# Normalising tiles as soon as they are complete, and writing out the middle groups of two attentions

## The chip, the core and the metric

The kernel runs on one core of a Trainium2 chip. The core has five engines that run side by side and wait for one another through semaphores: TensorE (PE in the profile; the loading of its weights is PEld), VectorE (DVE), ScalarE (ACT), GpSimd (POOL), and SyncE (SP), which here only issues DMA transfers. The metric is the time of one execution on the device, in microseconds (us).

## The reference, cut to what matters

Two decoder layers on 1024 tokens (4 sequences of 256) of width 512. Each layer is an attention and a feed-forward network, and after each of the four the residual sum is normalised over the 512 columns:

```
def _layernorm(x, axis=-1, eps=1e-05):
    m = jnp.mean(x, axis=axis, keepdims=True)
    v = jnp.var(x, axis=axis, keepdims=True)
    return (x - m) / jnp.sqrt(v + eps)

x = L0_attn_hidden_states
x = _layernorm(x + _L0_attn_ref(x, ...), axis=-1)   # 32 heads over a latent of 64, causal
x = _layernorm(x + _L0_ffn_ref(x, ...), axis=-1)    # weights unpacked from 4 bits (GPTQ)
x = _layernorm(x + _L1_attn_ref(x, ...), axis=-1)   # 32 heads and 32 latent heads, causal
x = _layernorm(x + _L1_ffn_ref(x, ...), axis=-1)    # weights rounded to 16 values per block of 64 (NF4)
```

## The kernel before

**Data.** `X` holds the tokens in SBUF as 8 tiles of 128 tokens by 512 columns (`TT` = 8), two tiles for each of the four sequences. `XT` is the same transposed. Every float32 matrix is held as a pair `hi` and `lo` (its rounded part and the rest), and each product is three matmuls (`product`, L59 to L65, so all of them carry lines 63, 64 and 65).

**Blocks.** The program is a row of blocks, and every engine meets every other at the end of each: an opening load; `transposed_block` (t0); the latent projections; the first attention (layer 0); `gptq_block`, which unpacks weights; `transposed_block` (t1); the first feed-forward; `transposed_block` (t2); `latent_query_block`; the second attention (layer 1), which also rounds the weights of the last feed-forward; `nf4_block`; `transposed_block` (t3); the second feed-forward; `transposed_block` (t4), which only normalises; and the store of the result.

**`transposed_block`** (L79 to L140). DVE takes the statistics of all eight tiles (L99, L102), adds epsilon (L104); ACT takes the root (L122); DVE takes the reciprocal (L106) and normalises the tiles in place (L109). PE transposes each tile in four matmuls (L139) as soon as it is normalised, into one of two PSUM banks; ACT copies the bank to `XT.hi` (L126), DVE writes the rest to `XT.lo` (L114), and only then is the bank free. t0 transposes without normalising.

**The attentions.** Both run over groups of heads, 4 groups in the first and 8 in the second, and each group over 16 steps (4 sequences by 4 heads or pairs of heads). A step n does the scores of n, the outputs of earlier steps, and projections for later ones. On every engine the first and the last group are written out, and the middle ones are a hardware loop, in which every count that a semaphore is compared with is computed in a register:

```
        def groups(eng, body):
            body(0, True, False)
            with eng.Fori(1, L0_GROUPS - 1) as g:
                body(g, False, False)
            body(L0_GROUPS - 1, False, True)
```

So the loop of the first attention runs twice and jumps back once, that of the second runs six times and jumps back five times. Where a wait needs a register, `hold` adds a semaphore increment behind it. After the last step of a sequence, `add_output` adds two tiles of the sum of a group to `X` (L759 in the first attention, L1396 in the second). In the last group this completes tiles 0 and 1 at step 6, 2 and 3 at step 10, 4 and 5 at step 14, and 6 and 7 at the very end.

**In the second attention**, POOL sums the terms of the rounded weights (L1076); at the first step of a group and at three later ones, DVE finishes a piece when POOL's sums are done (`code_end`, L1405) and starts the next (`code_start`), ahead of the reciprocal (L1378) that the step's softmax needs.

**The feed-forwards** (`ffn_block`) run over the two halves of the tokens; DVE adds the four tiles of the first half to `X` in the middle of the block (`add(0)`, unit 11 of 22) and the other four at its end.

Of the kernel before, what the change touches and what calls it, by code (L numbers as in the profile page):

```python
# [16 lines left out]
P = 128  # L17
# [61 lines left out]
def transposed_block(nc, tag, X, XT, ident, banks, signals, normed, flipped):  # L79


    with ExitStack() as ctx:  # L82
        sb = lambda n, s, d: ctx.enter_context(nc.sbuf_tensor(tag + n, s, d))
        stats = sb("stats", [P, TT, 6], F32)
        moments = sb("moments", [P, TT, 2], F32)
        root = sb("root", [P, TT], F32)
        inverse = sb("inverse", [P, TT], F32)
        stats_done, moments_done, var_ready, root_ready, inverse_done, x_ready, turned, hi_done, lo_done = signals
        normalise = normed is not None
        block = ctx.enter_context(nc.Block())  # L90

        def bank_view(t):
            return banks[t % 2][:, :].rearrange("p (k c) -> p k c", k=KT)

        @block.vector
        def _(dve):
            if normalise:
                for t in range(TT):
                    dve.bn_stats(stats[:, t, :], X[:, t, :]).then_inc(stats_done, 1)  # L99
                for t in range(TT):  # L100
                    dve.wait_ge(stats_done, TT * normed + t + 1)
                    dve.bn_aggr(moments[:, t, :], stats[:, t, :]).then_inc(moments_done, 1)  # L102
                dve.wait_ge(moments_done, TT * (normed + 1))
                dve.tensor_scalar(root[:, :], moments[:, :, 1], EPS, None, ALU.add).then_inc(var_ready, 1)  # L104
                dve.wait_ge(root_ready, normed + 1)
                dve.reciprocal(inverse[:, :], moments[:, :, 1]).then_inc(inverse_done, 1)  # L106
                dve.wait_ge(inverse_done, normed + 1)
                for t in range(TT):
                    dve.tensor_scalar(X[:, t, :], X[:, t, :], moments[:, t, 0:1], inverse[:, t:t + 1],  # L109
                                      ALU.subtract, ALU.mult).then_inc(x_ready, 1)  # L110
            if XT is not None:
                for t in range(TT):
                    dve.wait_ge(hi_done, TT * flipped + t + 1)
# [16 lines left out]
        def _(pe):  # L130
            if XT is None:
                return
            for t in range(TT):
                if normalise:
                    pe.wait_ge(x_ready, TT * normed + t + 1)
# [1799 lines left out]
```

## Time and profile before

| what | value |
|---|---|
| median of 3 timed runs | 2655.54 us (2655.51, 2655.54, 2663.71) |
| the profiled execution's own time | 2663.52 us |
| its span, first to last instruction | 2661.7 us |
| busy: PE, PEld, DVE, ACT, POOL | 89%, 78%, 66%, 55%, 59% |
| mean granted TensorE clock | 0.931 of full speed |
| idle of PE before t1, t2, t3 (from the last matmul before) | 9.02, 9.55, 7.67 us |
| from the last sum of the last feed-forward to the end of the span | 17.8 us |

The profile's page divides the span into 40 slices. PE is busy nearly throughout except in the slices of the opening, of the weight unpacking after the first attention, of the start of the second attention, of `nf4_block` and of the end. A line number such as L109 is a line of the kernel before. "x8" counts instructions, and what stands in square brackets is how long the engine was idle before, and which instruction ended that wait.

### The profile page before, as it was taken

How to read it: one execution, taken by the hardware profiler on the slowest of the kernel's cores; microseconds unless marked ns; L12 is line 12 of the kernel's file. 1: busy time of each engine (PE TensorE's matmuls, PEld its weight loads, DVE VectorE, ACT ScalarE, POOL GpSimd, SP SyncE). 2: the span in 40 equal slices, each digit the busy share in tenths (PEclk: the TensorE clock that was granted, in tenths of full speed). 3: DMA queues.
4: the chain of work that ended last, by engine and by line, in shares of the span. 5: the costliest groups of instructions: out<-in, count | busy, mean ns of one | idle time of the engine just before them, and what ended most of it. 6: DMA issues, size and time to landing. Idle time of an engine off the chain costs nothing. (4 is left out here: it accounts for less than half of the span.)

```text
span 2661.7 us, 44610 instructions
## 1 busy us (share of the span) xinstructions
PE 2371.4 (89%) x14333; PEld 2070.7 (78%) x14333; DVE 1756.2 (66%) x3123; ACT 1469.0 (55%) x3970; POOL 1564.7 (59%) x1320
## 2 busy tenths in 40 slices
PE   6699999996679957999999999999999999986996
PEld 5588888885358837889888888888888988875885
DVE  2366656664951136888888888888888888862123
ACT  1266656664033315666767767667676676764332
POOL 0636353631024408788787877878878878750542
PEclk8699989998579978999999999999999999997998
DMA  1201010101000012011111110111101111003000
GB/s 47 67 16 48 13 38 17 44 5 40 0 0 1 0 35 62 28 58 44 35 49 36 46 57 24 53 40 46 53 17 59 44 40 47 22 5 135 0 1 32
DMA packets 41237, 93.68 MB, mean 35 GB/s; under 512 B 4724, under 2 KB 6648, under 8 KB 39696
## 3 DMA queue, kind: packets, MB, share of 16 engines
q1 hardware_dynamic: 40980, 90.55, 10.6%
q8 instruction: 126, 2.06, 0.3%
q14 instruction: 131, 1.07, 0.1%
HBM read 79.78 MB, written 10.75 MB: 34 GB/s over the span
## 5 line engine op out<-in xcount | busy, mean ns | idle before, releaser
L1076 POOL TENSOR_TENSOR a_nf_acc<-a_nf_acc,a_nf_term 128x512 f32<-128x512 f32 (+1 forms) x416 | 587.5, 1412 | 141.3 <-ACT a_nf_term L1162 76.9
L1510 POOL TENSOR_TENSOR f_w_lo<-WGU,f_w_hi 128x512 fp32r<-128x512 f32 x88 | 113.1, 1288 | 370.5 <-ACT f_w_hi L1526 370.5
L1122 ACT ACTIVATE a_probs<-bank,a_dip 128x128 f32<-128x128 f32 (+1 forms) x512 | 208.8, 420 | 193.7 <-DVE a_dip L1372 193.7
L1131 ACT ACTIVATE a_probs<-a_probs,a_share 128x128 f32<-128x128 f32 (+1 forms) x512 | 191.9, 459 | 61.7 <-DVE a_share L1378 61.7
L1057 POOL TENSOR_TENSOR a_qk_lo<-a_straight,a_qk_hi 128x512 fp32r<-128x512 f32 (+1 forms) x160 | 194.5, 1217 | 32.1 <-ACT a_qk_hi L1108 32.1
L63 PE MATMUL bank<-a_wo_hi,a_ot_hi 128*128 128x512 f32 x512 | 212.7, 415 | 0.0
L1442 DVE TENSOR_SCALAR a_nf_term<-a_nf_unit 128x512 f32<-128x512 f32 (+1 forms) x288 | 205.4, 758 | 3.4 <-DVE a_nf_unit L1425 0.6
L1553 DVE TENSOR_TENSOR f_hidden<-bank,f_act_gate 128x512 f32<-128x512 f32 x44 | 30.4, 692 | 263.2 <-PE bank L65 257.2
L65 PE MATMUL bank<-a_wo_hi,a_ot_lo 128*128 128x512 f32 x512 | 201.3, 393 | 0.0
L64 PE MATMUL bank<-a_wo_lo,a_ot_hi 128*128 128x512 f32 x512 | 199.7, 390 | 0.0
L450 POOL TENSOR_TENSOR a_straight<-a_straight,a_crossed 128x512 f32<-128x512 f32 x64 | 82.5, 1289 | 191.0 <-DVE a_crossed L717 191.0
L1108 ACT ACTIVATE a_qk_hi<-a_straight 128x512 fp32r<-128x512 f32 (+1 forms) x160 | 94.5, 590 | 176.4 <-DVE a_straight L1357 176.4
L1263 PE MATMUL bank<-ident,a_probs 128*128 128x128 f32 x768 | 134.2, 284 | 50.5 <-DVE a_pt_lo L1383 49.6
L508 ACT ACTIVATE a_probs<-bank,a_dip 128x128 f32<-128x128 f32 (+1 forms) x256 | 104.3, 420 | 134.4 <-DVE a_dip L735 134.4
L63 PE MATMUL bank<-a_wvk_hi,XT_hi 128*128 128x320 f32 x512 | 169.5, 331 | 0.1
L1383 DVE TENSOR_TENSOR a_pt_lo<-bank,a_pt_hi 128x384 fp32r<-128x384 f32 x256 | 140.7, 550 | 40.4 <-ACT a_pt_hi L1139 40.4
L65 PE MATMUL bank<-a_wvk_hi,XT_lo 128*128 128x320 f32 x512 | 160.9, 314 | 0.0
L64 PE MATMUL bank<-a_wvk_lo,XT_hi 128*128 128x320 f32 x512 | 160.7, 314 | 0.0
L1357 DVE TENSOR_TENSOR a_straight<-a_straight,a_crossed 128x512 f32<-128x512 f32 (+1 forms) x160 | 153.9, 962 | 5.5
L1263 PEld LDWEIGHTS bank<-ident,a_probs 128*128 128x128 f32 x768 | 85.7, 142 | 83.6 <-DVE a_pt_lo L1383 74.8
L65 PE MATMUL bank<-XT_hi,a_wql_lo 128*128 128x256 f32 x512 | 146.5, 286 | 0.0
L64 PE MATMUL bank<-XT_lo,a_wql_hi 128*128 128x256 f32 x512 | 146.5, 286 | 0.0
(247 smaller groups left out, 8618.2 us busy)
## 6 DMA issues: line engine op xcount, KB each, us to landing
a_raw<-in_l_o SPq DMA_DIRECT2D x64, 256.0 KB, 2.6
a_raw<-in_l_vk SPq DMA_DIRECT2D x32, 384.0 KB, 3.1
a_raw<-in_l_ql SPq DMA_DIRECT2D x32, 320.0 KB, 2.9
a_raw<-in_l_ou SPq DMA_DIRECT2D x32, 288.0 KB, 2.7
n_codes<-coded_w SPq DMA_DIRECT2D x8, 1056.0 KB, 12.7
a_raw<-in_l_nr SPq DMA_DIRECT2D x16, 384.0 KB, 3.0
a_nf_raw<-in_w_nf SPq DMA_DIRECT2D x24, 256.0 KB, 2.6
coded_w<-a_nf_acc SPq DMA_DIRECT2D x24, 256.0 KB, 2.1
```

The lines of the kernel that those rows point to most:

```text
L63: pe.matmul(out, lh, rh, start=first, stop=False)
L64: pe.matmul(out, lh, rl, start=False, stop=False)
L65: return pe.matmul(out, ll, rh, start=False, stop=last)
L1057: pool.tensor_tensor(rope_cell(name, QK.lo), src, rope_cell(name, QK.hi).bitcast(F32), ALU.subtract)\
L1076: pool.tensor_tensor(acc, left, nf_term[:, i % CODE_RING, 0:w], ALU.add).then_inc(nf_added, 1)
L1122: act.activation(probs[:, n % 2, col:col + keys], bank[:, at:at + keys], ACT.Exp, bias=dip[:, n % 2, i:i + 1], accum_out=total[:, n % 2, i ...
L1131: ins = act.activation(cell, cell, ACT.Copy, scale=share[:, n % 2, i:i + 1])
L1263: last_ = pe.transpose(TURN[:, i * P:(i + 1) * P], probs[:, n % 2, col:col + P], ident[:, :])
L1357: dve.tensor_tensor(row, row, crossed[:, 0:n], ALU.add).then_inc(rope_sum, 1)
L1383: dve.tensor_tensor(PT.lo[:, at], TURN[:, 0:3 * P], PT.hi[:, at].bitcast(F32), ALU.subtract)\
L1442: dve.tensor_scalar(nf_term[:, i % CODE_RING, 0:w], nf_unit[:, 0:w], -BOUNDS[k], JUMPS[k], ALU.is_ge, ALU.mult).then_inc(nf_terms, 1)
L1510: pool.tensor_tensor(lo, src, hi.bitcast(F32), ALU.subtract).then_inc(part_lo[i], 1)
```

## The change

**Normalisation.** The buffers and semaphores of the normalisation now live through the whole program (`norm_buffers`), and its steps are functions (`measure`, `variance`, `deviation`, `normalise`) that take a range of tiles and a part, 0 or 1. In the last group of each attention DVE measures two tiles after each of three `add_output`s, ACT takes the root for six tiles in the tail of the group, and DVE normalises those six before its last `add_output`. In both feed-forwards DVE measures the four tiles of the first half at unit 11 and normalises them at unit 14. The `transposed_block`s normalise only what is left: two tiles in t1 and t3, four in t2. They use four PSUM banks in turn in place of two, and `low(0)` stands ahead of the normalisation. In the last feed-forward the first half of the result is stored while the second is computed, and `last_block` normalises the other four tiles and stores each as it is done.

**Groups.** In both attentions `for g in range(...)` stands in place of the hardware loop, on every engine: the middle groups are written out, with constants in place of registers, and `hold` adds no increment. `mask` of the second attention shares its place in SBUF with `probs`.

```diff
+def normalise(dve, X, norm, normed, part, tiles):
+    at = slice(tiles[0], tiles[-1] + 1)
+    dve.wait_ge(norm["root_ready"], 2 * normed + part + 1)
+    dve.reciprocal(norm["inverse"][:, at], norm["moments"][:, at, 1]).then_inc(norm["inverse_done"], 1)
+    dve.wait_ge(norm["inverse_done"], 2 * normed + part + 1)
+    for t in tiles:
+        dve.tensor_scalar(X[:, t, :], X[:, t, :], norm["moments"][:, t, 0:1], norm["inverse"][:, t:t + 1],
+                          ALU.subtract, ALU.mult).then_inc(norm["x_ready"], 1)
...
-            return banks[t % 2][:, :].rearrange("p (k c) -> p k c", k=KT)
+            return banks[t % 4][:, :].rearrange("p (k c) -> p k c", k=KT)
...
+            if normed is not None:
+                measure(dve, X, norm, normed, late)
+                variance(dve, norm, normed, late)
+                low(0)
+                normalise(dve, X, norm, normed, 1, late)
+            for t in range(0 if normed is None else 1, TT):
+                low(t)
...
+            high(0)
+            if normed is not None:
+                deviation(act, norm, normed, 1, late)
+            for t in range(1, TT):
+                high(t)
...
-                if t >= 2:
-                    pe.wait_ge(lo_done, TT * flipped + t - 1)
+                if t >= 4:
+                    pe.wait_ge(lo_done, TT * flipped + t - 3)
...
+def last_block(nc, X, out, norm, normed, stored):
+    late = range(TT // 2, TT)
...
+            for t in late:
+                sp.wait_ge(norm["x_ready"], TT * normed + t + 1)
+                sp.dma_start(out[t * P:(t + 1) * P, :], X[:, t, :]).then_inc(stored, 16)
...
         def groups(eng, body):
             body(0, True, False)
-            with eng.Fori(1, L0_GROUPS - 1) as g:
+            for g in range(1, L0_GROUPS - 1):
                 body(g, False, False)
             body(L0_GROUPS - 1, False, True)
...
+                    deviation(act, norm, normed, 0, range(TT - 2))
                     out_high(L0_STEPS - 1)
...
                         add_output(n - 3)
+                        if last and n > PAIRS:
+                            tiles = range(2 * (n // PAIRS) - 2, 2 * (n // PAIRS))
+                            dve.wait_ge(out_free, 2 * (BATCH * g + n // PAIRS))
+                            measure(dve, X, norm, normed, tiles)
...
                 if last:
+                    variance(dve, norm, normed, range(TT - 2))
                     out_low(L0_STEPS - 2)
                     for a in range(NP):
                         probs_low(L0_STEPS - 1, a)
                     out_low(L0_STEPS - 1)
+                    normalise(dve, X, norm, normed, 0, range(TT - 2))
                     add_output(L0_STEPS - 1)
...
-            with eng.Fori(1, GROUPS - 1) as g:
+            for g in range(1, GROUPS - 1):
...
+                if u == FT + 1:
+                    deviation(act, norm, normed, 0, range(HT))
...
                     add(0)
+                    dve.wait_ge(added, HT)
+                    measure(dve, X, norm, normed, range(HT))
+                if u == FT + 1:
+                    variance(dve, norm, normed, range(HT))
+                if u == FT + 3:
+                    normalise(dve, X, norm, normed, 0, range(HT))
```

DVE, block t1, before: the statistics, the normalisation and the low parts of all eight tiles stand in a row (`t_` names the block's own buffers).

```order
L99 BN_STATS t_stats<-X 128x6 x8
L102 BN_AGGR t_moments<-t_stats 128x2 x8
L104 TENSOR_SCALAR t_root<-t_moments 128x8
L106 RECIPROCAL t_inverse<-t_moments 128x8
L109 TENSOR_SCALAR X<-X,t_moments,t_inverse 128x512 x8
L114 TENSOR_TENSOR XT_lo<-bank,XT_hi 128x4x128 x8
```

DVE, the same block in the changed kernel (`ln_` names the shared buffers, lines are those of the changed kernel):

```order
L90 BN_STATS ln_stats<-X 128x6 x2
L93 BN_AGGR ln_moments<-ln_stats 128x2 x2
L100 TENSOR_SCALAR ln_root<-ln_moments 128x2
L137 TENSOR_TENSOR XT_lo<-bank,XT_hi 128x4x128
L115 RECIPROCAL ln_inverse<-ln_moments 128x2
L118 TENSOR_SCALAR X<-X,ln_moments,ln_inverse 128x512 x2
L137 TENSOR_TENSOR XT_lo<-bank,XT_hi 128x4x128 x7
```

Six of the eight tiles have left the block, and the first low part is ahead of the two that are normalised. They have gone, for t1, into the tail of the first attention. DVE there, in the changed kernel:

```order
L100 TENSOR_SCALAR ln_root<-ln_moments 128x6
L805 TENSOR_TENSOR a_ot_lo<-bank,a_ot_hi 128x256
L800 TENSOR_TENSOR a_pt_lo<-bank,a_pt_hi 128x384 x2
L805 TENSOR_TENSOR a_ot_lo<-bank,a_ot_hi 128x256
L115 RECIPROCAL ln_inverse<-ln_moments 128x6
L118 TENSOR_SCALAR X<-X,ln_moments,ln_inverse 128x512 x6
L813 TENSOR_TENSOR X<-bank,X 128x512 x2
```

The seven new instructions (reciprocal and six tiles) stand between the last `a_ot_lo` and the last sum. ACT, from the tail of the first attention to the first feed-forward, in the changed kernel:

```order
L584 ACTIVATE a_ot_hi<-bank 128x256
L578 ACTIVATE a_pt_hi<-bank 128x384 x2
L108 ACT_TABLE_LOAD
L108 ACTIVATE ln_moments<-ln_root 128x6
L584 ACTIVATE a_ot_hi<-bank 128x256
L368 UNCONDITIONAL_BRANCH
L149 UNCONDITIONAL_BRANCH
L153 ACTIVATE XT_hi<-bank 128x4x128
L108 ACTIVATE ln_moments<-ln_root 128x2
L153 ACTIVATE XT_hi<-bank 128x4x128 x7
```

The load of the table for the root has moved from the start of t1 into the attention's tail, and t1 itself has none.

## Rows read from the trace of the kernel before

**Rows 1.** Waits of PE: engine, line, waited for: us in total, times, longest
```profile
PE bank L139 <- DVE X L109: 26.2, 3, 9.5
PE bank L63 <- issue: 14.0, 6, 3.1
```

**Rows 2.** Timeline of t1: start us, us, engine, line, operation, count [idle before <-releaser]
```profile
745.86 4.84 DVE L99 BATCH_NORM_STATS2 t_stats<-X 128x6 f32<-128x512 f32 x8 [0.33 <-PEq L1596]
...
751.96 3.74 DVE L109 TENSOR_SCALAR X<-X,t_moments,t_inverse 128x512 f32<-128x512 f32 x8
752.56 1.99 PE L139 MATMUL bank<-ident,X 128*128 128x128 f32 x8 [9.02 <-DVE X L109]
753.73 0.60 ACT L126 ACTIVATE XT_hi<-bank 128x512 fp32r<-128x512 f32 x1 [2.04 <-PE bank L139]
754.59 0.60 ACT L126 ACTIVATE XT_hi<-bank 128x512 fp32r<-128x512 f32 x1 [0.26 <-PE bank L139]
755.62 1.28 DVE L114 TENSOR_TENSOR XT_lo<-bank,XT_hi 128x512 fp32r<-128x512 f32 x2
...
764.28 0.69 DVE L114 TENSOR_TENSOR XT_lo<-bank,XT_hi 128x512 fp32r<-128x512 f32 x1 [0.16 <-ACT XT_hi L126]
```

**Rows 3.** Timeline of t0, its start and its last low part
```profile
9.92 1.28 ACT L126 ACT_TABLE_LOAD   x1 [9.92 <-PEq L1788]
...
20.33 0.69 DVE L114 TENSOR_TENSOR XT_lo<-bank,XT_hi 128x512 fp32r<-128x512 f32 x1 [0.16 <-ACT XT_hi L126]
```

**Rows 4.** DMA issues: out<-in, queue, count, KB each, us to landing
```profile
coded_w<-a_nf_acc SPq DMA_DIRECT2D x24, 256.0 KB, 2.1
...
out_x<-X SPq DMA_DIRECT2D x1, 2048.0 KB, 7.0
```

**Rows 5.** Timeline of DVE, tail of the first attention
```profile
646.16 0.42 DVE L751 TENSOR_TENSOR a_ot_lo<-bank,a_ot_hi 128x256 fp32r<-128x256 f32 x1 [3.21 <-ACT a_ot_hi L531]
648.54 1.29 DVE L759 TENSOR_TENSOR X<-bank,X 128x512 f32<-128x512 f32 x2 [1.95 <-PE bank L65]
```

**Rows 6.** Timeline of DVE, tail of the second attention
```profile
2399.17 0.75 DVE L1405 SCALAR_TENSOR_TENSOR a_nf_acc<-a_nf_acc,a_nf_top 128x576 f32<-128x576 f32 x1
2403.43 1.29 DVE L1396 TENSOR_TENSOR X<-bank,X 128x512 f32<-128x512 f32 x2 [3.52 <-PE bank L65]
```

**Rows 7.** Windows (length, busy and count by engine, clock): second attention, last group; first feed-forward
```profile
2286.60:2328.70 42.10, 40.66 (x274) 36.85 (x273) 38.26 (x67) 31.18 (x86) 31.21 (x24) 1.00 0.05 15
...
860.00:900.00 40.00, 40.00 (x178) 33.10 (x178) 9.41 (x14) 13.72 (x25) 19.36 (x15) 1.00 0.00 1
```

**Rows 8.** Windows in the first attention: step 15 to step 1, and steps 4 to 11
```profile
360.59:386.70 26.11, 23.26 (x121) 20.15 (x120) 11.24 (x24) 10.84 (x35) 14.18 (x21) 0.74 0.13 36
501.95:519.68 17.73, 17.29 (x121) 14.74 (x120) 11.13 (x24) 10.93 (x35) 11.74 (x16) 1.00 0.13 35
140.30:201.38 61.08, 59.46 (x402) 50.35 (x402) 40.16 (x76) 40.16 (x129) 23.80 (x23) 1.00 0.02 7
272.84:334.46 61.62, 59.50 (x403) 50.40 (x402) 40.16 (x76) 40.16 (x129) 23.73 (x22) 1.00 0.03 8
```

**Rows 9.** Windows in the second attention, step 15 to step 13 of the next group
```profile
1346.25:1499.45 153.20, 145.54 (x960) 133.50 (x959) 130.46 (x231) 103.06 (x284) 120.87 (x96) 0.98 0.13 40
...
2034.20:2186.62 152.42, 144.23 (x960) 132.02 (x959) 131.66 (x231) 103.13 (x284) 120.40 (x96) 0.99 0.13 40
2205.49:2359.99 154.50, 145.44 (x961) 133.02 (x959) 134.28 (x231) 102.89 (x284) 112.33 (x90) 0.98 0.08 27
1174.08:1327.38 153.30, 144.07 (x961) 131.84 (x960) 131.70 (x231) 103.15 (x284) 120.68 (x96) 0.99 0.12 39
```

**Rows 10.** Timeline of DVE and PE at two group boundaries of the second attention
```profile
1364.48 1.31 DVE L1405 SCALAR_TENSOR_TENSOR a_nf_acc<-a_nf_acc,a_nf_top 128x576 f32<-128x576 f32 x1
...
2223.29 1.83 DVE L1405 SCALAR_TENSOR_TENSOR a_nf_acc<-a_nf_acc,a_nf_top 128x576 f32<-128x576 f32 x1 [2.10 <-POOL a_nf_acc L1076]
...
2228.87 0.90 PE L1263 MATMUL bank<-ident,a_probs 128*128 128x128 f32 x3 [3.98 <-DVE a_pt_lo L1383]
```

More of the change, by code:

```diff
@@ L90, in transposed_block @@
+def transposed_block(nc, X, XT, ident, banks, signals, norm, normed, flipped, early):
+    with ExitStack() as ctx:
+        turned, hi_done, lo_done = signals
+        late = range(early, TT)
         block = ctx.enter_context(nc.Block())
         def bank_view(t):
-            return banks[t % 2][:, :].rearrange("p (k c) -> p k c", k=KT)
+            return banks[t % 4][:, :].rearrange("p (k c) -> p k c", k=KT)
         @block.vector
         def _(dve):
[L97 to L110, printed above, removed]
@@ L123, in _, with high @@
-            if XT is not None:
-                for t in range(TT):
-                    act.wait_ge(turned, TT * flipped + t + 1)
-                    act.activation(XT.hi[:, :, t * P:(t + 1) * P], bank_view(t), ACT.Copy)\
-                       .then_inc(hi_done, 1)
+            def high(t):
+                act.wait_ge(turned, TT * flipped + t + 1)
+                act.activation(XT.hi[:, :, t * P:(t + 1) * P], bank_view(t), ACT.Copy)\
+                   .then_inc(hi_done, 1)
+            high(0)
@@ L1462, in body @@
                         add_output(n - 3)
+                        if last and n > PER:
+                            tiles = range(2 * (n // PER) - 2, 2 * (n // PER))
+                            dve.wait_ge(out_free, 2 * (BATCH * g + n // PER))
+                            measure(dve, X, norm, normed, tiles)
                     for name in units[1:]:
@@ L1465, in body @@
                 if last:
+                    variance(dve, norm, normed, range(TT - 2))
                     out_low(STEPS - 2)
@@ L1470, in body, with ffn_block @@
                     code_end(PER - 1)
+                    normalise(dve, X, norm, normed, 0, range(TT - 2))
                     add_output(STEPS - 1)
             groups(dve, body)
-def ffn_block(nc, tag, X, XT, banks, WGU, WD):
+def ffn_block(nc, tag, X, XT, banks, WGU, WD, norm, normed, out, stored):
     with ExitStack() as ctx:
@@ L1539, in _ @@
                 split_high(u + 1, 2)
+                if u == FT + 1:
+                    deviation(act, norm, normed, 0, range(HT))
+        if out is not None:
+            @block.sync
+            def _(sp):
+                sp.wait_ge(norm["x_ready"], TT * normed + HT)
+                sp.dma_start(out[0:HALF, :].rearrange("(t p) d -> p t d", p=P), X[:, 0:HT, :]).then_inc(stored, 16)
         @block.vector
```

101 lines of the change are left out of this document (57 added, 44 removed).

## The prediction, as recorded before the changed kernel was run

> **What bounds the kernel now.** I read the page's busy shares first (PE 89%), then PE's waits, since what does not shorten a wait of PE, or the work behind it, does not shorten the program. Three waits of that list are touched. PE waits for `X` at the start of t1, t2 and t3, 26.2 us in all, and six times, 14.0 us in all, for "issue", that is for nothing the profile shows [rows 1]. Six is also the number of backward jumps (one in the first attention, five in the second), and those waits lie at the group boundaries. The timelines of the transposing blocks come next: in each, DVE works through eight tiles while PE and ACT stand still, then the two banks make PE, ACT and DVE take turns [rows 2]. The end of the program is a fourth such place: the chain that ended last is DVE's normalisation of all eight tiles, then the store. Last, I cut the attentions into windows with the same work, some across a boundary with a jump and some across one without.
>
> **t1 and t3.** Before, the block runs from 745.86 to 764.28 + 0.69 = 764.97: 19.1 us [rows 2]. Afterwards PE can begin at once, for six tiles are ready. The eight transposes of two tiles take 1.99 us; ACT's first copy starts 753.73 - 752.56 = 1.17 after them and the next 0.86 later. So copy t starts at 1.2 + 0.86t, the eighth at 7.2, ends at 7.8, and DVE's low part (0.69) ends near 8.5. DVE does not delay it: two statistics (4.84 / 8 = 0.6 each) make 1.2; all from there to the first normalised tile was 751.96 - 745.86 - 4.84 = 1.26 for eight tiles, so no more for two; two tiles are 0.46 each (3.74 / 8) and eight low parts 0.6 each (1.28 for two): 1.2 + 1.3 + 0.9 + 4.8 = 8.2, and they run beside PE. Four banks keep PE from waiting for `lo`. Gain 10.6 each, 21.2 for both. If PE's clock rises within the block it is half a microsecond more, and if DVE's parts collide it is a microsecond less.
>
> **t0** gains by the banks alone. It starts at 9.92, with a table load of 1.28 beside the first transposes, and ends at 21.02 [rows 3]; at the spacing above the eighth copy starts at 9.9 + 7.3 = 17.2 and the low part ends at 18.4. Gain 2.6.
>
> **t2** keeps four tiles. DVE sets its length: four statistics 2.4, at most 1.3 to the first normalised tile less the copies that need not wait, `low(0)` 0.6 between, four tiles 1.9, seven low parts 4.3: about 10.2, of a block that was as long as t1 before. Gain 8.9.
>
> **The end.** From the first statistic to the landing of the result were 17.2 us: DVE's 9.9, a block boundary of 0.3, and the 2048 KB store with 7.0 [rows 4]. Afterwards four statistics (2.4) and at most 1.3 bring the first normalised tile to start at 3.6 and end at 4.1, the others follow 0.46 apart. A 256 KB store took 2.1 us; from 2048 KB at 7.0, each further 256 KB costs (7.0 - 2.1) / 7 = 0.7. Four in a row: 4.1 + 2.1 + 3 x 0.7 = 8.3. Gain 8.9. The store of the first half is hidden in the feed-forward, which moves nearly nothing by DMA.
>
> These give 2.6 + 21.2 + 8.9 + 8.9 = 41.6 us.
>
> **What they cost elsewhere.** In the tail of the first attention, DVE was free at 646.58 and PE's last sum came at 648.54 [rows 5]. The reciprocal and six tiles take 0.2 + 0.05 + 6 x 0.46 = 3.0, so the last sum starts at 649.6 in place of 648.54: 1.1 us later, and the loads of the next block, issued behind the boundary, with it. In the tail of the second attention the same 3.0 us start at 2399.92 and end at 2402.9, before 2403.43, when PE is done: nothing, with 0.5 us of cover [rows 6]. If it isn't there, it costs what it overruns by. The table for the root (1.28 us [rows 3]) loads while ACT waits for PE's last products: DVE's wait of 3.21 us for ACT's last copy [rows 5] is that gap. Measuring two tiles costs DVE 1.5 us, three times in each attention. In the first, DVE works 40.16 of 61 us over eight steps [rows 8], so it is hidden. In the second it works 38.26 of 42.10 [rows 7], and PE 40.66: a delay there partly reaches PE. Bounds 0 and 3 x 1.5 = 4.5; I take 1, since step 14 has room and a softmax has a step of slack. In the feed-forwards PE is busy all 40.00 of 40.00 us with DVE at 9.41 and ACT at 13.72 [rows 7]: measuring, normalising and two more table loads vanish there; uncovered, the loads would be 2 x 1.28 in each. So the normalisation nets 41.6 - 1.1 - 1.0 = 39.5.
>
> **Writing out the first attention.** From step 15 to step 1 takes 26.11 us across the jump and 17.73 across the boundary without one, with the same 121 matmuls. The granted clock over the stretch is 0.74 against 1.00 [rows 8]: the wait for issue is a third of it at most (3.1 is the longest of the six), the rest is work at 1.2 GHz, which PE got after it had stood still. Gain 8.4. Besides, eight steps take 61.62 with registers and 61.08 without: 0.07 a step, 30 steps, 2 us, and a further 1 for slower first steps. Together 11.4.
>
> **Writing out the second attention.** The same cut does not show a gain. From step 15 to step 13 of the next group, the five boundaries with a jump (the first and the last are shown) took 153.0 in the mean; the two without took 153.3 and 154.5, the latter with constants throughout [rows 9]. The reason shows at two of the boundaries [rows 10]: at the first step DVE has to finish a piece of the rounded weights when POOL's sums are done. Without a jump DVE waits 2.10 us for POOL and finishes the piece at 2225.12, 19.6 after step 15 began (2205.49); with the jump it arrives late, the sums are there, and it finishes at 1365.79, 19.5 after 1346.25. PE merely gets there sooner and waits 3.98 us in one piece; the clock over that group is 0.98. So no gain; I take the mean of the two excesses, 0.3 and 1.5: 0.9 x 5 = 4.6 us lost. Bounds: 0 and 7.5.
>
> On these jumps the Trainium skill ("Runtime: NRT & Kernel Launch", Instruction fetch mechanics) says that a taken branch out of the prefetched window stalls the engine until the target page is fetched, and that kernels are better fully unrolled for it. That such a stall exists the trace agrees with (the six waits); by the rule all 14.0 us would come back, 11.4 of them in the second attention, which the windows speak against [rows 9]. That is a rival below.
>
> **Sum.** 39.5 + 11.4 - 4.6 = 46.3. Against the profiled execution's own 2663.52 this is 2617.2. That execution is 8.0 us above the median of the timed runs, 2655.54, so the median would be 2609.2. What made it 8 us slower isn't known; it may be the slow clock after the jump of the first attention (0.26 x 26.1 = 6.8 us of lost clock), and then the median has less to gain. I allow 0.8 for it: 2610.
>
> **The rivals.**
> 1. *All jumps pay* (chance 0.12): the waits for issue in the second attention come back in full. For it: they are in PE's list. Against: both groups of rows on it [rows 9, 10]. It would turn -4.6 into +11.4: 2594.
> 2. *The gain is partly eaten* (0.13): DVE in the last group of the second attention is full, so measuring costs 4.5, the boundaries cost 7.5, and the first attention's jump is worth only its wait of 2.6 plus 3. 41.6 - 1.1 - 4.5 + 5.6 - 7.5 = 34.1, and with the transposing blocks a microsecond longer each, 30: 2625. For it: the two boundaries without a jump are two samples only.
> 3. *Slower than before* (0.02): PE's single pause of 4 us, now at all seven boundaries of the second attention in place of two, is followed by a long stretch at 1.2 GHz. The price: PE is busy 40.66 of 42.10 us there [rows 7], so that 24 us at the lower level would cost about 12. It decides from 46.3 / 5 = 9.3 us on for each of the five new boundaries; at 12 each the time is 2610 + 60 = 2670. Against it: the two such boundaries that exist cost 0.3 and 1.5.
>
> **How the numbers follow.** My forecast, 2610, has a chance of 0.73, the rivals 0.12, 0.13 and 0.02. The firm part is the 39.5 of the normalisation, which rests on idle time of PE with nothing behind it; the unknown parts are the second attention (0 to 7.5 lost, or 11.4 gained), the measuring (0 to 4.5) and the first attention's jump (2.6 to 8.4). Adding the unfavourable ends with half weight each gives some 2624, the favourable ones without rival 1 some 2602; to leave out no more than 2 in 10 the range takes in rivals 1 and 2 nearly whole: 2595 to 2626. About 0.3% (8 us) is what a measurement of this kernel can tell from no change. All cases but the third, and a remainder, are faster by more than that: faster 0.97, within it 0.01, slower 0.02.
>
> **What would show it.** In the profile after: t1 and t3 some 8.5 us long from their first transposes to their last low part, with PE starting at once and in one piece, t2 10.2, t0 8.5; no table load in t1 and t3 and one pair more in each feed-forward, with PE at full share beside it; the last sum of the first attention 3.0 us after its last low part, that of the second still released by PE. The last store lands some 8.3 us after the last block's first statistic. In the first attention, step 15 to step 1 takes 17.7 at the former jump, at clock 1.00, and eight steps 61.0. In the second, PE has one wait of 4 us for `a_pt_lo` at each boundary, DVE waits 2 us for POOL before `code_end`, and step 15 to step 13 takes 153 to 154.5 us everywhere. The prediction is wrong if the groups of the second attention become shorter or longer than that by more than 2 us, if PE's waits for `issue` stay, or if the transposing blocks don't begin with PE.

## The result and the profile after

The changed kernel takes 2629.9 us (median of 4 runs, 2629.7 to 2635.3), the kernel before 2659.6 us in the same session (4 runs, 2655.5 to 2664.8): ratio 0.9902, 95% interval 0.9885 to 0.9919 (the quotient of these two medians, 0.9888, lies inside it). It is faster by 1.0%, not by the 1.7% forecast, and lies 4 us above the top of the range. The profiled execution of the changed kernel took 2629.9 us too, so its blocks can be set beside those of the profiled execution before (2663.5), from the start of one block to the start of the next:

| block | before | after | change | predicted |
|---|---|---|---|---|
| t0 | 11.4 | 7.5 | -3.9 | -2.6 |
| first attention | 581.3 | 571.5 | -9.9 | -10.3 |
| t1 | 19.4 | 8.1 | -11.4 | -10.6 |
| first feed-forward | 186.2 | 190.1 | +4.0 | 0 |
| t2 | 19.4 | 10.5 | -8.9 | -8.9 |
| second attention | 1418.8 | 1431.5 | +12.8 | +5.6 |
| t3 | 19.4 | 7.9 | -11.5 | -10.6 |
| second feed-forward | 186.4 | 191.2 | +4.8 | 0 |
| last normalisation and store | 17.6 | 8.5 | -9.1 | -8.9 |
| all others together | | | -0.5 | 0 |
| sum | | | -33.6 | -46.3 |

The waits of PE in the profile after (us in total, times, longest) answer to [rows 1]:

```profile
PE bank L1324 <- DVE a_pt_lo L1444: 70.6, 53, 4.1
...
PE bank L63 <- POOL a_wql_lo L1108: 23.7, 1, 23.7
```

The waits for issue are gone from the list, and those for `X` are down to 0.7 us, in t2. The wait for the low part of the turned probabilities in the second attention has grown from 49.6 us in 39 to 70.6 us in 53.

Timeline of t1, which answers to [rows 2]:

```profile
732.51 1.28 DVE L90 BATCH_NORM_STATS2 ln_stats<-X 128x6 f32<-128x512 f32 x2 [0.32 <-PEq L1677]
732.51 6.23 PE L170 MATMUL bank<-ident,X 128*128 128x128 f32 x32 [2.31 <-PEq L1677]
...
735.08 1.00 DVE L118 TENSOR_SCALAR X<-X,ln_moments,ln_inverse 128x512 f32<-128x512 f32 x2
...
736.00 4.27 DVE L137 TENSOR_TENSOR XT_lo<-bank,XT_hi 128x512 fp32r<-128x512 f32 x7
```

PE starts with the block and works in one piece; DVE's statistics and two tiles lie beside it. The last low part ends at 740.27, 7.8 after the start (predicted 8.5).

DVE in the tails of the first and of the second attention, which answers to [rows 5, 6]:

```profile
632.20 0.42 DVE L805 TENSOR_TENSOR a_ot_lo<-bank,a_ot_hi 128x256 fp32r<-128x256 f32 x1 [2.10 <-ACT a_ot_hi L584]
...
632.77 2.83 DVE L118 TENSOR_SCALAR X<-X,ln_moments,ln_inverse 128x512 f32<-128x512 f32 x6
635.51 1.28 DVE L813 TENSOR_TENSOR X<-bank,X 128x512 f32<-128x512 f32 x2
...
2382.15 2.83 DVE L118 TENSOR_SCALAR X<-X,ln_moments,ln_inverse 128x512 f32<-128x512 f32 x6
2385.54 1.29 DVE L1457 TENSOR_TENSOR X<-bank,X 128x512 f32<-128x512 f32 x2 [0.56 <-PE bank L65]
```

Both sums stand as forecast: the first held back by the six tiles, the second still released by PE.

Windows of the changed kernel (length; busy time and count of PE, PEld, DVE, ACT, POOL; granted clock), in the first attention step 15 to step 1 at the former jump and steps 4 to 11 [rows 8], in the second step 15 to step 13 at the second boundary and at the last [rows 9]:

```profile
354.16:371.80 17.64, 17.29 (x121) 14.74 (x120) 11.13 (x24) 10.92 (x35) 11.71 (x16) 1.00 0.13 35
...
267.35:328.27 60.92, 59.52 (x402) 50.43 (x402) 40.15 (x76) 40.11 (x129) 23.70 (x22) 1.00 0.02 8
...
1317.98:1473.07 155.09, 144.70 (x960) 131.87 (x959) 135.58 (x231) 102.96 (x284) 119.89 (x96) 0.98 0.12 39
...
2182.53:2339.13 156.60, 143.98 (x960) 131.59 (x959) 136.31 (x239) 103.11 (x284) 112.91 (x90) 0.98 0.08 27
```

The first two are the forecast's 17.7 and 61.0 at clock 1.00. The five former jumps of the second attention take 152.9 to 155.1 (forecast 153 to 154.5). The last boundary takes 156.6, which is 2.1 more than that range and more than the 154.5 before: two of the new measurings lie in this stretch. At one of them, which answers to [rows 10], DVE waits for POOL's sums with the softmax queued behind it, and PE waits for DVE:

```profile
1335.78 1.84 DVE L1466 SCALAR_TENSOR_TENSOR a_nf_acc<-a_nf_acc,a_nf_top 128x576 f32<-128x576 f32 x1 [2.12 <-POOL a_nf_acc L1136]
...
1341.36 0.90 PE L1324 MATMUL bank<-ident,a_probs 128*128 128x128 f32 x3 [4.10 <-DVE a_pt_lo L1444]
```

The issues of the last store (KB each, median us to landing) answer to [rows 4]; the first half's store is hidden, and from the first statistic to the end of the span pass 2628.1 - 2619.6 = 8.5 us (predicted 8.3):

```profile
out_x<-X SPq DMA_DIRECT2D x1, 1024.0 KB, 4.4
out_x<-X SPq DMA_DIRECT2D x4, 256.0 KB, 2.4
```

**Three things the forecast did not have.** First, in the last groups: DVE after step 6 of the second attention, and PE's waits about that place.

```profile
2274.03 1.28 DVE L1457 TENSOR_TENSOR X<-bank,X 128x512 f32<-128x512 f32 x2
2275.34 1.29 DVE L90 BATCH_NORM_STATS2 ln_stats<-X 128x6 f32<-128x512 f32 x2
2276.54 0.30 DVE L93 BATCH_NORM_AGGREGATE ln_moments<-ln_stats 128x2 f32<-128x6 f32 x2
2276.76 0.46 DVE L1422 TENSOR_TENSOR a_vl_lo<-bank,a_vl_hi 128x320 fp32r<-128x320 f32 x1
```
```profile
PE bank L1324 <- DVE a_pt_lo L1444: 1.6, 1, 1.6
```

The step after it takes 11.38 us where it took 9.86, and the step after the second measuring 13.24 where it took 11.79: the 1.42 us that measuring two tiles needs come through in full. In the first attention the same two steps grew from 7.62 to 8.62 and from 7.61 to 8.61.

Second, in the feed-forwards, with clock 1.00 in both: 40 us of the first one, before [rows 7] and after.

```profile
840.00:880.00 40.00, 40.00 (x174) 32.34 (x173) 16.41 (x27) 17.14 (x28) 18.83 (x15) 1.00 0.00 1
```

PE is busy all the time, yet gets through 174 matmuls where it did 178. From unit to unit it takes 8.34 us in place of 8.16. The gate functions of ACT keep the same pace but for the two beside the table loads, 9.00 and 7.68, which is the same in sum. So it is not the measuring, which stands in the middle of the block.

Third, the ends of the second attention: from its start to the first scores 35.7 us where it was 32.6, and from the last scores to its end 33.5 where it was 30.5.

### The profile page after: what moved, and what is told of

It reads as the page before. It is cut to its first block and busy times, and to the rows that moved or that the text cites. A ratio compares the mean times of both kernels' runs of the same rounds, so it can differ in the third digit from the quotient of the medians.

```text
span 2628.1 us, 40095 instructions
## 1 busy us (share of the span) xinstructions
PE 2360.5 (90%) x14333; PEld 2054.7 (78%) x14333; DVE 1788.2 (68%) x3131; ACT 1472.4 (56%) x3978; POOL 1560.8 (59%) x1320
## 3 DMA queue, kind: packets, MB, share of 16 engines
q1 hardware_dynamic: 41044, 90.55, 10.5%
## 5 line engine op out<-in xcount | busy, mean ns | idle before, releaser
L1503 DVE TENSOR_SCALAR a_nf_term<-a_nf_unit 128x512 f32<-128x512 f32 (+1 forms) x288 | 228.4, 838 | 1.1
L1628 DVE TENSOR_TENSOR f_hidden<-bank,f_act_gate 128x512 f32<-128x512 f32 x44 | 30.5, 693 | 256.4 <-PE bank L65 240.5
L1324 PE MATMUL bank<-ident,a_probs 128*128 128x128 f32 x768 | 135.9, 287 | 71.9 <-DVE a_pt_lo L1444 70.6
L63 PE MATMUL bank<-XT_hi,f_w_hi 128*128 128x512 f32 x352 | 140.9, 400 | 7.7 <-POOL f_w_lo L1577 7.7
L63 PE MATMUL bank<-XT_hi,a_wql_hi 128*128 128x256 f32 x512 | 143.2, 280 | 0.0
## 6 DMA issues: line engine op xcount, KB each, us to landing
n_codes<-coded_w SPq DMA_DIRECT2D x8, 1056.0 KB, 12.7
```

Of the source, the lines that this page charges most:

```text
L63: pe.matmul(out, lh, rh, start=first, stop=False)
L1324: last_ = pe.transpose(TURN[:, i * P:(i + 1) * P], probs[:, n % 2, col:col + P], ident[:, :])
L1503: dve.tensor_scalar(nf_term[:, i % CODE_RING, 0:w], nf_unit[:, 0:w], -BOUNDS[k], JUMPS[k], ALU.is_ge, ALU.mult).then_inc(nf_terms, 1)
```

## The experiments

Times are compared as ratios to the kernel before, run beside each kernel (its medians were 2655.6 to 2655.9 us in these sessions). The number to compare with is the changed kernel's 0.9902. Four further kernels were executed once each and are read by their blocks: the kernel before with other gaps (2662.4 and 2661.9 us), the kernel before in the new placement (2664.9), and the changed kernel with the loop of the first attention (2630.0).

| kernel | us | ratio, 95% interval |
|---|---|---|
| changed, gap before the feed-forwards' weights | 2621.7 | 0.9867 (0.9851 to 0.9884) |
| changed, loop kept in the second attention | 2621.1 | 0.9865 (0.9849 to 0.9882) |
| changed, normalising in the unpacking blocks | 2614.5 | 0.9849 (0.9830 to 0.9868) |
| changed, codes behind the softmax at step 0 | 2615.0 | 0.9846 (0.9826 to 0.9867) |
| gap, unpacking blocks and codes together | 2593.8 | 0.9766 (0.9747 to 0.9785) |
| the same with the loop kept | 2606.6 | 0.9813 (0.9790 to 0.9837) |
| together, codes behind at 4 steps | 2623.6 | 0.9887 (0.9865 to 0.9909) |
| together, codes behind at all steps | 2733.9 | 1.0289 (1.0268 to 1.0310) |

**The feed-forwards: placement.** The new buffers take 320 bytes per partition ahead of the weights.

```diff
+            scope.enter_context(nc.sbuf_tensor("gap0", [P, 48], F32))
             WGU = scope.enter_context(nc.sbuf_tensor("WGU0", [P, KT, 2 * FT * P], F32))
```

> The changed kernel with 192 unused bytes per partition ahead of the weight buffers of both feed-forwards, so that with the 320 bytes of the statistics they lie 512 bytes further than before the change, not 320. Theory (placement): the feed-forwards' units go back from 8.34 to 8.16 us, 190.2 and 191.2 back to about 186.2 and 186.5, the whole from 2629.9 to 2621 us. Rival (the measuring, the square root and its table loads inside the feed-forwards cost it): units stay at 8.34 us, the whole stays at 2630 us.

The same gap stands ahead of `WGU1`. Units took 8.16 us, the feed-forwards 187.2 and 187.2: the theory holds for the units. The blocks stayed about a microsecond above the 186.2 and 186.4 before, which the units do not explain. Rows of PE in 40 us of the first (total, mean ns), in the changed kernel and with the gap:

```profile
L63 PE MATMUL bank<-XT_hi,f_w_hi 128*128 128x512 f32 x40 | 15.8, 394 | 0.0
```
```profile
L63 PE MATMUL bank<-XT_hi,f_w_hi 128*128 128x512 f32 x39 | 15.2, 389 | 0.0
```

The reverse, on the kernel before, with gaps of 320 and 64 bytes:

```diff
+            scope.enter_context(nc.sbuf_tensor("gap0", [P, 80], F32))
             WGU = scope.enter_context(nc.sbuf_tensor("WGU0", [P, KT, 2 * FT * P], F32))
...
+            scope.enter_context(nc.sbuf_tensor("gap1", [P, 16], F32))
             WGU = scope.enter_context(nc.sbuf_tensor("WGU1", [P, KT, 2 * FT * P], F32))
```

> The kernel before the change, with nothing but unused bytes per partition ahead of the feed-forwards' weight buffers: 320 in the first, 64 in the second. Theory (placement): the first takes 190.2 us instead of 186.2; the second tells which step of the address counts: also about 190.2 if 64 bytes off are as bad as 320, 186.4 if not. Rival (placement does nothing): 186.2 and 186.4, the whole within 0.1% of 2659.6 us.

Both feed-forwards took 8.34 us a unit, 190.0 and 190.3 in all. Nothing else had been changed, so placement alone makes the slow units. Then with `[P, 32]` and `[P, 64]` in the same two lines:

> The kernel before the change, with unused bytes per partition ahead of the feed-forwards' weight buffers: 128 in the first, 256 in the second. At 320 and 64 a unit took 8.34 us, at 0 and 512 it took 8.16. If only the place within 512 bytes counts, both are 8.34 (feed-forwards 190.2); if the place within 128 counts, both are 8.16 (186.3); if that within 256, the first is 8.34 and the second 8.16.

At 128 bytes a unit took 8.33 us, at 256 it took 8.16 (189.8 and 186.7). So of the offsets tried 0, 256 and 512 are good, and 64, 128 and 320 bad. The intervals between the matmuls that hold the gate and up weights and stream `XT` grew from 0.227 to 0.233 us; most of those of the down product stayed. The gap moves the block's other buffers with the weights, and what in the core makes the difference was not tried.

**Placement of everything, without the new code.**

```diff
+        ctx.enter_context(nc.sbuf_tensor("gap", [P, 80], F32))
         signals = [ctx.enter_context(nc.semaphore("t_" + n)) for n in
...
-        mask = sb("mask", [P, P], F32)
+        mask = probs[:, 0, 0:P]
```

> The kernel before the change, with 320 unused bytes per partition ahead of everything but X and XT, and with the mask of the second attention laid into the probabilities' buffer: the placement of the changed kernel, and none of its code. Theory (placement costs the feed-forwards only): feed-forwards 190.1 and 190.2 us; second attention start to first scores 32.7, groups 1 to 6 1031, tail 30.4, as before the change. Rival (placement also made the second attention later): start to first scores 34 to 36 us, or groups 1 to 6 at 1035 us and more.

Feed-forwards 190.3 and 190.4; second attention: start 32.7, groups 1 to 6 1030.5, tail not longer. The theory holds. Its steps 2 to 4 became shorter, 9.60 to 9.52 us, as in the changed kernel, so that is placement too; the groups did not.

The start of the second attention took 32.6 to 33.1 us in the four profiled executions of the old code, and 33.0 to 35.7, 33.8 in the mean, in ten of the new. So some 1 us of the 3.1 belongs to the change, and the rest to that execution; the transfers that POOL waited for were slower in it (its second piece of `in_l_vk` landed 6.4 us after its issue, in the others 4.6 to 5.3). What the 1 us is stays open. The block ahead of it, `latent_query_block`, gives back more: it took 15.2 to 15.7 us in the four executions of the old code and 12.7 to 13.1 in nine of the ten of the new (14.4 in the profile of the changed kernel). Its weights landed 2.7 to 3.0 us after their issue, before 3.9 to 4.4, and in those nine PE's clock over the rest of the block was 0.77 to 0.80, before 0.68 to 0.70. The forecast had no term for it.

**Normalising where DVE is idle.**

```diff
-                            measure(dve, X, norm, normed, tiles)
...
-                    variance(dve, norm, normed, range(TT - 2))
...
-                    normalise(dve, X, norm, normed, 0, range(TT - 2))
...
+            normalise_all(dve, X, norm, normed)
             dve.wait_ge(landed, 176)
```

(`normalise_all` measures and normalises eight tiles; it also stands behind the two `memset`s of `nf4_block`.)

> The changed kernel without any normalising in the attentions' last groups; all 8 tiles are normalised at the start of the block that unpacks the next weights instead, where VectorE is idle (first 13.5 us of the first such block, nearly all 33 us of the second), so both transposing blocks behind them only transpose. Theory (VectorE is short in the last groups, and what was put there costs its whole length): first attention 571.5 to 568.0 (two steps back from 8.62 to 7.62, tail 20.4 to 18.9), second 1431.5 to 1425.6 (steps 11.38 and 13.24 back to 9.86 and 11.79, tail 33.4 to 30.5), transposing blocks 8.07 and 7.92 to 7.5, unpacking blocks unchanged: the whole 2619.5 us. Rival (those steps and tails are longer for another reason, placement or code fetching): attentions unchanged, the whole 2629 us.

The steps went back to 7.61 and 7.62, 9.85 and 11.73; the tails to 18.4 and 30.5; the attentions to 565.0 and 1423.7, which is 3.0 and 1.9 less than expected; the unpacking blocks took 95.5 and 32.3, no longer than before. DVE at the start of the first of them:

```profile
629.22 4.24 DVE L90 BATCH_NORM_STATS2 ln_stats<-X 128x6 f32<-128x512 f32 x7
...
636.57 1.92 DVE L118 TENSOR_SCALAR X<-X,ln_moments,ln_inverse 128x512 f32<-128x512 f32 x4
642.07 2.40 DVE L1729 MEMSET WD<- 4x2816 uint32 x1 [3.58 <-DMA q_tail_shift<-in_shift_d]
```

All eight tiles are done 3.6 us before the transfers that DVE would have waited for anyway.

The tails can be compared over all profiled executions. That of the first attention takes 18.4 us without normalising where the clock does not fall in it, 19.9 where it is low for 3.4 us, and 20.9 for 6.8 (before: 20.9). With the normalising it takes 22.4 at 3.4 us of low clock and 24.3 to 24.8 at 10.2. So the edit costs 2.5 us at the same clock. The last sum's wait for DVE is 0.9 of that; another 1.5 is a pause of PE that grew from 1.6 to 3.1 us where it waits for the softmax of step 15, which is queued behind the measuring of step 14. Where the table load stands, ACT is idle as forecast. The profile of the changed kernel flatters this tail: 22.4 us there, 24.3 to 24.8 in the other four kernels with the normalising, against 19.9 to 20.9 in four executions of the old code.

The tail of the second attention takes 30.2 to 31.9 us in nine executions without the normalising and 33.1 to 33.5 in four of five with it (30.9 in the fifth). Its last sum waits for PE in both, so the cost comes from somewhere else. DVE behind step 14 and the pause of PE that follows, in the changed kernel and with the normalising moved:

```profile
2358.08 1.29 DVE L90 BATCH_NORM_STATS2 ln_stats<-X 128x6 f32<-128x512 f32 x2
2359.28 0.30 DVE L93 BATCH_NORM_AGGREGATE ln_moments<-ln_stats 128x2 f32<-128x6 f32 x2
2359.49 0.99 DVE L1433 TENSOR_REDUCE a_dip<-bank 128x2 f32<-128x256 f32 x2
...
2368.14 0.58 PE L63 MATMUL bank<-a_pt_hi,a_vl_hi 128*128 128x256 f32 x1 [3.62 <-DVE a_pt_lo L1444]
```
```profile
2342.98 1.28 DVE L1465 TENSOR_TENSOR X<-bank,X 128x512 f32<-128x512 f32 x2
2344.18 1.01 DVE L1441 TENSOR_REDUCE a_dip<-bank 128x2 f32<-128x256 f32 x2
...
2352.86 0.39 PE L63 MATMUL bank<-a_pt_hi,a_vl_hi 128*128 128x256 f32 x1 [3.11 <-DVE a_pt_lo L1452]
```

It is the same as in the first attention: the measuring stands ahead of the peaks (`a_dip`) of step 15, and its softmax comes later. From the scores of step 15 (2353.6 and 2339.8) the peaks start after 5.9 us in place of 4.4, and PE's matmuls behind the pause after 14.6 in place of 13.1. That is 1.5 of the 3 us. The rest goes with the clock: in the four executions the lower level holds for 3.4 and 10.2 us of the tail, in all nine without the normalising for 10.2 in sum. In the fifth it holds for 6.8, with the same pauses.

**The loop of the first attention.**

```diff
-            for g in range(1, L0_GROUPS - 1):
+            with eng.Fori(1, L0_GROUPS - 1) as g:
```

> The changed kernel with the engine loop put back in the first attention alone. Theory (what the first attention won comes from writing out): its two middle groups take 274.7 us instead of 262.9, the whole 11.8 us more, 2641.7. Rival (it comes from placement or from what surrounds it): 263 us stay.

The middle groups took 270.7 us, 7.8 more than written out, so most of the gain is shown to be the writing out, but not all 11.9. The stretch across the jump, in the kernel before [rows 8] at clock 0.74, was here:

```profile
354.83:376.85 22.02, 18.89 (x120) 16.08 (x120) 11.13 (x24) 10.83 (x35) 11.74 (x16) 0.92 0.11 29
```

4.4 us over the written-out 17.64, with clock 0.92. In four profiled executions of the old code it took 26.0 to 26.1 at 0.74. Behind the pause the lower level held for 13.7 us in each of those four and for 3.4 here; why is open. The waits against registers show as well: steps 4 to 11 take 61.63 us with the loop and 60.92 without, 0.09 a step. The whole took 2630.0 us in its one execution, no more than the changed kernel. Its first attention is 10.9 us longer, and other blocks are shorter by as much (second attention 4.6, latent projections 3.2, `nf4_block` 2.2), which is the scatter of a single execution. So this gain is read from the block and not from the whole.

**The loop of the second attention.**

```diff
-            for g in range(1, GROUPS - 1):
+            with eng.Fori(1, GROUPS - 1) as g:
```

> The changed kernel with the engine loop put back in the second attention alone. Theory (straight-line code costs more there than the jumps did): its six middle groups take 1031.4 us again instead of 1036.8, the whole falls by about 5, to 2625 us. Rival (the jumps' 14.0 us of issue on TensorE were the price, and the 12.8 us that the second attention lost come from elsewhere): the middle groups take up to 14 us longer, the whole is up to 2644 us.

Groups 1 to 6 took 1030.9 us, and the ratio fell from 0.9902 to 0.9865, of which the groups are 0.22 points; the rest was not placed. Written out they took 1036.5 to 1037.3 in four kernels. The theory holds.

**DVE's wait at the boundary.** If the pause of PE comes from the piece of rounded weights that stands ahead of the softmax, it should vanish where that piece stands behind it.

```diff
                     peaks(n)
-                    codes(n)
+                    held = n == 0 and not first
+                    if not held:
+                        codes(n)
                     shares(n)
...
                         probs_low(n - 1, 0)
+                    if held:
+                        codes(n)
```

> The changed kernel with one step of VectorE moved: at the first step of each group but the first of the second attention, the rounded weights' piece is finished and the next one begun behind the low part of the first turned probabilities, not ahead of the shares. Theory (VectorE's wait of 2.1 us for GpSimd's sums, with the softmax queued behind it, makes TensorE's one pause of 4.0 us at each boundary, and the low clock of 3.4 to 6.8 us that follows it costs half its length): 4 to 6 us less at each of seven boundaries, groups 1 to 6 at about 1010 us in place of 1036.8, the whole about 2602 us. Rival (VectorE is full there, the 5 us of work come later and hold the next rotation as long): groups 1 to 6 stay within 5 us of 1036.8, the whole at 2630 us.

Groups 1 to 6 took 1023.7 us: 13 less, half of what was expected, with every group at 170.6. Both theories missed the number. DVE at the boundary:

```profile
1334.82 0.18 DVE L1439 RECIPROCAL a_share<-a_total 128x4 f32<-128x4 f32 x1 [1.78 <-ACT a_probs L1182]
...
1336.38 0.75 DVE L1466 SCALAR_TENSOR_TENSOR a_nf_acc<-a_nf_acc,a_nf_top 128x576 f32<-128x576 f32 x1
```

DVE now waits 1.78 us for ACT's exponentials in place of 2.12 us for POOL, and the sums are there when it comes to them. Step 0 falls from 15.0 or more to 9.6 us, and step 1 rises from 11 or more to 13.9, since the rotation of the next queries now stands behind the codes; step 5 gives back up to another microsecond. No stretch of low clock is left between the first group and the last. In the next kernel, with the same code in these groups, 3.4 us of it came back in each, at step 5; why is open.

The next two kernels take the three edits together (the gap, the unpacking blocks, the codes at step 0), written out and with the loop.

> The changed kernel with three edits together: the gap ahead of the feed-forwards' weights, the normalising at the start of the unpacking blocks, and the rounded weights' piece taken behind the softmax at the group boundaries. Gap and normalising alone should give 2610 us; with the first theory on the boundaries 2583 us, with its rival 2610 us.

> The same as the kernel with all three edits, and the engine loop kept in the second attention. Theory (VectorE's wait decides what the jumps are worth): with the wait gone, writing out pays as in the first attention, and this kernel is slower than the written-out one, by up to 14 us (five jumps at 2.3 to 2.8 us of issue each): 2583 + 14 = 2597 us. Rival (straight-line code costs 5 to 6 us by itself there): this one is faster by 6 us.

2593.8 us written out and 2606.6 with the loop: 12.7 us, the first theory's side. The 2583 us of its other half was missed, as in the run before. Groups 1 to 6 took 1025.1 and 1041.1. The same edit took 12 us off the written-out groups and put 10 on the looped ones. In the looped kernel DVE had waited for POOL at step 0 in one of the six groups only (2.07 us), for behind a jump it came late; written out it waited in all six (2.06 to 2.12). So in the loop the edit had hardly a wait to remove. The windows from step 15 to step 2 of the next group (the boundary behind group 1) show the four cases, one kernel each: changed; changed with the loop; codes behind the softmax, written out; the same with the loop (and the other two edits).

```profile
1317.98:1357.61 39.63, 33.50 (x209) 30.43 (x208) 32.28 (x51) 22.26 (x61) 29.66 (x25) 0.91 0.13 42
```
```profile
1319.41:1356.50 37.09, 31.01 (x210) 27.87 (x208) 29.89 (x52) 22.24 (x61) 29.98 (x24) 1.00 0.15 49
```
```profile
1317.34:1352.94 35.60, 31.23 (x209) 27.84 (x208) 30.89 (x50) 21.59 (x60) 28.81 (x24) 1.00 0.14 47
```
```profile
1303.97:1342.87 38.90, 32.82 (x210) 29.37 (x208) 31.26 (x50) 21.92 (x61) 29.29 (x24) 0.96 0.14 46
```

The third takes 35.6 us, at clock 1.00, at six of its seven boundaries and 35.9 at the last. The first has 38.1 to 39.6 at 0.91 to 0.96: beside the pause itself, the low clock behind it.

**More of the same.**

```diff
-                    held = n == 0 and not first
+                    held = n in (0, 5, 8, 11) and not (first and n == 0)
```

> The kernel with all three edits (2593.8 us), where the rounded weights' piece is taken behind the softmax not only at the first step of a group but at all four steps at which a piece ends (0, 5, 8 and 11). Theory (VectorE's wait for GpSimd's sums holds the softmax at these too): step 5 falls from 13.4 to 14.9 us to about 10.5, steps 8 and 11 by 1 us each, groups 1 to 6 from 1025 to about 1000, the whole 2570 us. Rival (VectorE is full in these steps, only the order changes): what one step wins the next loses, 1025 us, the whole 2594 us.

Worse than either: groups 1 to 6 took 1051.0 us. Step 5 stayed at 13.4 to 14.9 us, step 8 fell from 10.6 to 9.5, and steps 9 and 11 rose from 11.2 to 14.1 to 14.5 and from 12.3 to 14.0 to 14.9. PE's waits, with the codes behind at step 0 only and at four steps:

```profile
PE bank L1332 <- DVE a_pt_lo L1452: 45.0, 45, 2.7
...
PE bank L63 <- DVE a_crossed L1423: 22.1, 17, 1.6
```
```profile
PE bank L63 <- DVE a_crossed L1423: 65.2, 41, 2.2
...
PE bank L1332 <- DVE a_pt_lo L1452: 31.7, 33, 2.1
```

13.3 us of the wait for the softmax went, and 43.1 us of wait for the rotation came. With the codes behind at step 0 only, DVE did not wait for POOL at steps 8 and 11 of these groups. At step 5 it did, 1.5 us in each:

```profile
1376.37 1.75 DVE L1474 SCALAR_TENSOR_TENSOR a_nf_acc<-a_nf_acc,a_nf_top 128x512 f32<-128x512 f32 x1 [1.54 <-POOL a_nf_acc L1145]
```

Moving the codes took this wait away, yet step 5 took no less than in the two kernels that have it (13.4 and 14.9 us). So the wait for POOL is not the whole account of where the move pays; what else decides it was not isolated.

> The same with the codes behind the softmax in every step. Theory: as the one with four steps or a little better, 2565 to 2570 us. Rival (at the other steps the codes fill a wait of VectorE for the exponentials, 1.8 us where they were moved away): 12 more steps lose up to 1.8 us each, groups 1 to 6 up to 100 us longer, slower than 2594 us.

1129.5 us for groups 1 to 6, the rival's side and its size: the wait for the rotation is 117.4 us in 78.

## Why the prediction was wrong, step by step

The forecast was 19.9 us too low. Two of its terms failed above all: the feed-forwards, put at nothing, cost 8.8 us, and the measuring, put at 1 us, cost 5.0 and lengthened both tails besides.

**Confirmed.** t1, t3, t2 and the end came within a microsecond of their working, t0 gained 1.3 more than forecast. The six tiles ahead of the last sum hold the first attention's end and not the second's. Writing out the first attention gave 11.9 us at the place named (11.4 forecast), of which putting the loop back shows 7.8. Writing out the second lost 5.3 (4.6 forecast), and the loop put back gives it back. "All jumps pay" was rightly set against [rows 9, 10], and the mechanism read there (DVE's 2.10 us for POOL, PE's 3.98) is borne out: with the codes moved behind the softmax the jumps do cost 12.7 us.

**Wrong, 8.8 us:** "measuring, normalising and two more table loads vanish there". They do, but the step took the feed-forwards for as long as before, because what is added to them is hidden, and the new buffers moved their weights by 320 bytes. The slower units are 22 x 0.18 = 4.0 us in each; the other 0.8 is in the second and not explained. Nothing in the sum asked where buffers come to lie.

**Wrong, 4.0 us:** "Measuring two tiles costs DVE 1.5 us [...] In the first [...] it is hidden [...] I take 1". It cost 2.0 in the first attention and 3.0 in the second. DVE's busy share of 40.16 in 61 us [rows 8] was taken for room, but its idle time lies in waits for the same softmax that the measuring holds up: where it was put, each step is a chain through DVE. Step 14, named as the one with room, made the softmax of step 15 1.5 us late in both tails as well, which is counted below.

**Wrong, 3.0 us:** "nothing, with 0.5 us of cover" for the tail of the second attention. The last sum was covered. The tail is longer all the same, by 1.5 us through the measuring behind step 14 and by as much again with more time at the lower clock. In the first attention 1.1 was forecast and 1.5 seen, but at equal clock it is 2.5, and in four other executions 3.4 us and more: the pause behind step 14 had been left out.

**Not in the sum, 3.1 us** at the start of the second attention, some 2 of them scatter, as above. The gain of `latent_query_block` was not in it either (1.0 in this profile; in the other nine 2.3 to 2.7 below the old code's mean of 15.4).

These make 8.8 + 4.0 + 3.0 + 3.1 = 18.9. The transposing blocks and the end gave back 3.2, the start of the first attention 1.3, the other steps of the second attention's last group 1.2, and the other blocks 0.5: 18.9 - 6.2 = 12.7, which is 46.3 - 33.6.

**The other 7.2 us of the 19.9** stand between the profiled executions and the medians. The old kernel's profiled execution lay 8.0 us above the median shown, and the forecast took that off, all but 0.8; the changed kernel's profile lies on its median. For a forecast of medians that subtraction was right. What it means is that the table above flatters the change: by the ratio it saved 26 us (2629.9 against the 2655.6 to 2655.9 of the later sessions), and not 33.6. The old kernel's runs went from 2651.5 to 2664.8 us over all sessions, and its profiled execution was a long one: its first attention took 581.3 us (578.2 to 579.8 in three others of its code), its second 1418.8 (1414.8 to 1417.9). The changed kernel's profile had luck in the first attention: 571.5 us, and 574.4 to 575.2 in three others with the same code there. In the mean of four each that block gained some 6 us, where 10.3 was forecast: its tail cost 2.4 more than forecast and its two longer steps 2.0.

The rival that came nearest was the second, partly eaten, at 2625: the reasons it gave were partly right (measuring) and partly not (jumps worth less, boundaries dearer). What the third described happened too, a pause of 4 us at all seven boundaries with 3.4 or 6.8 us of low clock behind each, but it cost 5.3 to 5.9 us over groups 1 to 6 and not 60.

## What to carry to other kernels

A change that adds a small buffer moves every buffer behind it: see to it that the big operands move by an amount that leaves the matmuls their pace (256 and 512 bytes did here, 64, 128 and 320 did not), or price the matmuls anew. Work is free where its engine waits for something outside the chain, as DVE did for transfers in the unpacking blocks, and not where its busy share is merely below one. And two waits of one place hide each other: over groups 1 to 6, writing the loop out alone lost 5 us, moving the codes behind the softmax with the loop kept 10 us, and both together won 6 (1031.5, 1036.8, 1041.1, 1025.1).

## What the runs showed of the hardware

- The matmuls of 128x512 for gate and up came every 0.227 us or every 0.233 us, at clock 1.00 in both, by the offset of the buffers alone: 8.16 or 8.34 us a unit of 36 matmuls, 2% of a feed-forward.
- The granted clock fell to its lower level (1.2 GHz) for 3.4 or 6.8 us after single pauses of PE of 4 us in a stretch where it was otherwise busy, at all seven boundaries of the changed kernel, and did not fall there once the pause was gone.
- The same jump cost 8.4 us at clock 0.74 in one program and 4.4 us at 0.92 in another.
